# Attention with a top-31 threshold on one core: scores stored less a per-row constant, and the step between two counts taken out

## The reference, cut to what matters

```python
U = min(L, int(FACTOR * math.log(L)))            # 31
scores = jnp.einsum('bhqd,bhkd->bhqk', Q, K) / math.sqrt(D)
top_vals, _ = jax.lax.top_k(scores, U)
thresh = top_vals[..., -1:]
scores = jnp.where(scores < thresh, -jnp.inf, scores)
attn = jax.nn.softmax(scores, axis=-1)
context = jnp.einsum('bhqk,bhkd->bhqd', attn, V)
...
x = _layernorm(x + attention(x)); x = _layernorm(x + ffn(x))
```

## Time and profile before

| | us |
|---|---|
| median of 3 executions | 3479.99 (3476.94 to 3483.20) |
| profiled execution | 3479.86 |
| its span, first to last instruction | 3478.0 |
| granted TensorE clock, mean | 0.897 of full speed |

### The profile page before, as it was taken

The page is one execution under the profiler, slowest core; times in us unless marked ns, Lnnn a source line. Parts: engine busy times, 40 slices in busy tenths (PEclk is TensorE's granted clock), DMA queues, the critical chain, the costliest instruction groups (busy, mean ns, idle before and its releaser), DMA issues.

```text
span 3478.0 us, 83180 instructions
## 1 busy us (share of the span) xinstructions
PE 2872.5 (83%) x21439; PEld 1516.8 (44%) x21439; DVE 2716.7 (78%) x13407; ACT 2336.1 (67%) x5894; POOL 2372.2 (68%) x1549
## 2 busy tenths in 40 slices
PE   5889999697889888866998997988969887787886
PEld 2344545344444444433544453444535444343454
DVE  5888888788878877777887887887878877777861
ACT  3777777585767676655776776766757765576662
POOL 2777778576777766654777786776757765575782
PEclk6899999898999988887999998998979998899886
DMA  2101011110101111011010111101011110110000
GB/s 81 41 20 42 23 40 30 32 26 18 43 23 34 24 34 31 19 32 22 21 44 23 33 26 37 33 25 37 23 32 26 33 33 18 32 26 24 22 14 7
DMA packets 91073, 102.85 MB, mean 30 GB/s; under 512 B 34417, under 2 KB 52850, under 8 KB 90482
## 3 DMA queue, kind: packets, MB, share of 16 engines
q1 hardware_dynamic: 88448, 93.73, 11.2%
q10 hardware_dynamic: 2034, 2.76, 0.2%
HBM read 20.86 MB, written 8.39 MB: 8 GB/s over the span
## 4 chain that ended last, share of the span: by engine, by line
PE 42%; DVE 24%; issue 17%; ACT 9%; DVEq 5%; POOL 2%; SPq 1%; ACTq 1%; DMA 0%; POOLq 0%
DVE cand L855 7%; PE Y_ps L593 6%; PE bench L657 5%; PE bench L663 5%; PE Y_ps L590 4%; PE ctxT_ps L621 4%; PE ST_ps L607 4%; ACT junk L447 4%; PE ST_ps L604 3%; PE Y_ps L591 3%; DVE S L841 3%; DVEq L935 3%; ACT above L455 3%; DVE gtop L916 2%; PE bench L650 2%
## 5 line engine op out<-in xcount | busy, mean ns | idle before, releaser
L1073 POOL TENSOR_SCALAR mask<-S,thr,mb 128x512 bf16<-128x512 f32 x1024 | 2112.1, 2075 | 44.0 <-POOL mb L1067 34.9
L447 ACT ACTIVATE junk<-S,nt 128x512 bf16<-128x512 f32 x1024 | 733.7, 716 | 563.7 <-DVE S L841 549.4
L855 DVE MAX8 cand<-Y_ps 128x8 f32<-128x128 f32 x4096 | 1074.2, 283 | 0.4
L841 DVE TENSOR_SCALAR_CACHE_REDUCE S<-S_ps 128x512 f32<-128x512 f32 x1024 | 702.7, 686 | 275.5 <-PE S_ps L580 216.7
L590 PE MATMUL Y_ps<-ones_b,nbig 128*128 128x512 bf16 x1024 | 421.6, 412 | 521.4 <-DVE cand L855 330.3
L463 ACT ACTIVATE PT<-ST_ps 128x512 f32<-128x512 f32 x1024 | 595.9, 582 | 234.2 <-PE ST_ps L607 233.3
L455 ACT ACTIVATE above<-S,nt 128x512 bf16<-128x512 f32 x1024 | 726.4, 709 | 0.2 <-DVE nt L848 0.2
L1067 POOL TENSOR_SCALAR mb<-rmax 128x8 f32<-128x8 f32 x128 | 31.1, 243 | 894.8 <-DVEq L938 894.8
L580 PE MATMUL S_ps<-KS,QS 64*128 64x512 f32 x1024 | 540.3, 528 | 2.0 <-DMA KS<-Klo 1.4
L593 PE MATMUL Y_ps<-KS,QS 64*128 64x512 f32 x1024 | 539.9, 527 | 0.0
L604 PE MATMUL ST_ps<-QS,KS 64*128 64x512 f32 x1024 | 439.7, 429 | 29.0 <-ACT PT L463 27.2
(11 more groups left out here) (119 smaller groups left out, 4005.4 us busy)
## 6 DMA issues: line engine op xcount, KB each, us to landing
QS<-Qhi SPq DMA_DIRECT2D x512, 32.0 KB, 2.0
KS<-Khi SPq DMA_DIRECT2D x512, 32.0 KB, 2.0
KS<-Klo SPq DMA_DIRECT2D x512, 32.0 KB, 2.0
QS<-Qlo SPq DMA_DIRECT2D x512, 32.0 KB, 2.0
xTs<-in_xT SPq DMA_DIRECT2D x17, 512.0 KB, 3.7
xs<-in_x SPq DMA_DIRECT2D x16, 512.0 KB, 3.9
out<-xs SPq DMA_DIRECT2D x16, 512.0 KB, 2.9
hT<-in_wgT ACTq DMA_DIRECT2D x1, 768.0 KB
```

Of the source, the lines that this page charges most:

```text
L447: nc.scalar.activation(junk[:, :], S[:, score_place(j)[0], :], ACT.Sign, bias=nt0[:, hb, col:col + 1], accum_out=s0[:, j % 8:j % 8 + 1]).t ...
L841: nc.vector.tensor_scalar(S[:, at, :], S_ps[n % 2][:, :], 1.0, None, ALU.mult, op1=ALU.max, accum_out=rmax[:, n % RING:n % RING + 1]).then ...
L855: mx = nc.vector.max(cand[:, j % CANDS, i, :], Y_ps[j % 2][:, i * BW:(i + 1) * BW])
L1073: nc.gpsimd.tensor_scalar(mask[:, h % MASKS, t, :], S[:, score_place(j)[0], :], thr[:, r:r + 1], mb[:, r:r + 1], ALU.is_lt, op1=ALU.add).t ...
```

## The change

Scores are stored with the row constant `na` already added: evacuate becomes S = S_ps + na, `na` read as a per-partition operand in place of the immediate 1.0. `na` is the second threshold's constant part, so the first count needs a bias `nt0` that is a multiple of the deviation alone, and takes its input with a scale of -1. The second threshold test S + s0*nb + na > 0 becomes steep * S - (count) > 0: ScalarE's second count reads the per-row factor `steep` = 4 / (BETA * sd2) as its scale and the first count's own output `s0` as its bias. VectorE's `aim` is dropped. The lag of the second count goes from 3 to 2, its wait from `aimed_done` to `cnt0_done`; all later lags stay. `evacuate` now waits for `stat_done` at tiles 0 and 32 of a batch. VectorE's moments end with one more reciprocal (`rsd2`). As thresholds and masks must be in the same terms, `pick_threshold` writes its result to `least` and adds `na` of the 8 tiles into `thr` (one more VectorE instruction in 8 tiles, which `check` waits for), and GpSimd makes `mb` in two steps in place of one, rmax / 2^40 and then plus `back` = -na / 2^40. `first_thresholds` keeps five instructions, the last of which now also depends on the fourth.

```diff
-AIMED = 2
-COUNT1 = 3
+COUNT1 = 2
...
-                nc.scalar.activation(junk[:, :], S[:, score_place(j)[0], :], ACT.Sign, bias=nt0[:, hb, col:col + 1],
+                nc.scalar.activation(junk[:, :], S[:, score_place(j)[0], :], ACT.Sign, bias=nt0[:, hb, col:col + 1], scale=-1.0,
                                      accum_out=s0[:, j % 8:j % 8 + 1]).then_inc(cnt0_done, 1)
...
-                act.wait_ge(aimed_done, T - COUNT1 + 1)
+                hb, col = j // HALF_TILES, (j % NT) * HALF + j // NT % HALF
+                act.wait_ge(cnt0_done, T - COUNT1 + 1)
                 if not (first and n < COUNT1 + 4):
                     act.wait_ge(below_done, T - COUNT1 - 3)
-                nc.scalar.activation(above[:, j % 4, :], S[:, score_place(j)[0], :], ACT.Sign, bias=nt1[:, j % 8:j % 8 + 1],
-                                     accum_out=s1[:, j % RING:j % RING + 1]).then_inc(cnt1_done, 1)
+                nc.scalar.activation(above[:, j % 4, :], S[:, score_place(j)[0], :], ACT.Sign, bias=s0[:, j % 8:j % 8 + 1],
+                                     scale=steep[:, hb, col:col + 1], accum_out=s1[:, j % RING:j % RING + 1]).then_inc(cnt1_done, 1)
...
-                    nc.vector.tensor_tensor(sd2[:, :], sd0[:, :], sd1[:, :], ALU.add).then_inc(sd_done, 1)
-
-            def evacuate(T, n, first):
+                    m = mark(nc.vector.tensor_tensor(sd2[:, :], sd0[:, :], sd1[:, :], ALU.add))
+                    dve.wait_ge(dve_step, m)
+                    nc.vector.reciprocal(rsd2[:, :], sd2[:, :]).then_inc(sd_done, 1)
+
+            def evacuate(T, n, b, first):
+                hb, col = n // HALF_TILES, (n % NT) * HALF + n // NT % HALF
+                if n % HALF_TILES == 0:
+                    dve.wait_ge(stat_done, b * 2 + hb + 1)
...
-                nc.vector.tensor_scalar(S[:, at, :], S_ps[n % 2][:, :], 1.0, None, ALU.mult, op1=ALU.max,
+                nc.vector.tensor_scalar(S[:, at, :], S_ps[n % 2][:, :], na[:, hb, col:col + 1], None, ALU.add, op1=ALU.max,
                                         accum_out=rmax[:, n % RING:n % RING + 1]).then_inc(s_copied, 1)
...
-            def aim(T, n):
-                j = (n - AIMED) % TILES
-                hb, col = j // HALF_TILES, (j % NT) * HALF + j // NT % HALF
-                dve.wait_ge(cnt0_done, T - AIMED + 1)
-                nc.vector.tensor_scalar(nt1[:, j % 8:j % 8 + 1], s0[:, j % 8:j % 8 + 1], nb[:, hb, col:col + 1],
-                                        na[:, hb, col:col + 1], ALU.mult, op1=ALU.add).then_inc(aimed_done, 1)
...
-                t = mark(nc.vector.tensor_reduce(thr[:, r:r + PAIR], picked[:, :, :], AX.X, ALU.max))
+                t = mark(nc.vector.tensor_reduce(least[:, :], picked[:, :, :], AX.X, ALU.max))
...
+                picks["kept"] = mark(nc.vector.tensor_tensor(by_head(thr[:, r:r + PAIR]), by_head(least[:, :]), of_pair(na, g), ALU.add))
...
+                if "kept" in picks:
+                    dve.wait_ge(dve_step, picks["kept"])
                 dve.nop(nofuse=True).then_inc(thr_done, 1)
...
-                    nc.gpsimd.tensor_scalar(mb[:, r:r + PAIR], rmax[:, r:r + PAIR], 1.0 / BIG, None,
-                                            ALU.mult).then_inc(mb_done, 1)
-                    wait_apart(pool, mb_done, pair + 1)
+                    nc.gpsimd.tensor_scalar(rbig[:, :], rmax[:, r:r + PAIR], 1.0 / BIG, None, ALU.mult).then_inc(mb_done, 1)
+                    wait_apart(pool, mb_done, 2 * pair + 1)
+                    nc.gpsimd.tensor_tensor(by_head(mb[:, r:r + PAIR]), by_head(rbig[:, :]),
+                                            of_pair(back, (n - MASK) // PAIR % NP), ALU.add).then_inc(mb_done, 1)
+                    wait_apart(pool, mb_done, 2 * pair + 2)
...
+                nc.gpsimd.tensor_scalar(asd[:, :], sd2[:, :], -ZERO / 2, None, ALU.mult).then_inc(stat_step, 1)
+                nc.gpsimd.tensor_scalar(nt0[:, hb, :], sd2[:, :], -(ZERO - Z) / 2, None, ALU.mult).then_inc(stat_step, 1)
+                nc.gpsimd.tensor_scalar(steep[:, hb, :], rsd2[:, :], 4.0 / BETA, None, ALU.mult).then_inc(stat_step, 1)
+                wait_apart(pool, stat_step, n0 + 1)
+                nc.gpsimd.tensor_tensor(na[:, hb, :], nmean[:, :], asd[:, :], ALU.add).then_inc(stat_step, 1)
                 wait_apart(pool, stat_step, n0 + 4)
+                nc.gpsimd.tensor_scalar(back[:, hb, :], na[:, hb, :], -1.0 / BIG, None, ALU.mult).then_inc(stat_done, 1)
```

More of the change, by code:

```diff
@@ L37 @@
 BETA = SHRINK / (L * float(np.exp(-Z * Z / 2) / np.sqrt(2 * np.pi)))
+ZERO = Z2 + BETA * (L / 2 - EXPECTED)
 BLOCKS = 4
@@ L212, in build @@
         rsd = sb("rsd", [P, NT * HALF])
-        zsd = sb("zsd", [P, NT * HALF])
+        rsd2 = sb("rsd2", [P, NT * HALF])
         asd = sb("asd", [P, NT * HALF])
@@ L216, in build @@
         na = sb("na", [P, 2, NT * HALF])
-        nb = sb("nb", [P, 2, NT * HALF])
+        back = sb("back", [P, 2, NT * HALF])
+        steep = sb("steep", [P, 2, NT * HALF])
         V = sb("V", [P, NT, NG, VG])
@@ L237, in build @@
         mb = sb("mb", [P, RING])
+        rbig = sb("rbig", [P, PAIR])
         thr = sb("thr", [P, RING])
@@ L240, in build @@
         s0 = sb("s0", [P, 8])
-        nt1 = sb("nt1", [P, 8])
         above = sb("above", [P, 4, L], BF16)
@@ L248, in build @@
         picked = sb("picked", [P, PAIR, RANKS])
+        least = sb("least", [P, PAIR])
         hidden = sb("hidden", [P, PAIR])
@@ L281, in build @@
         cnt0_done = sem("cnt0_done")
-        aimed_done = sem("aimed_done")
         cnt1_done = sem("cnt1_done")
@@ L315, in build, with of_pair, by_head @@
         block = ctx.enter_context(nc.Block())
+        def of_pair(a, g):
+            h = 2 * g % HALF
+            return a[:, 2 * g // HALF, :].rearrange("p (t h) -> p h t", h=HALF)[:, h:h + 2, :]
+        def by_head(a):
+            return a.rearrange("p (h t) -> p h t", h=2)
         def wait_apart(eng, s, value):
@@ L899, in pick_threshold @@
             def pick_threshold(n):
-                g = (n - THRESHOLD) // PAIR
+                g = (n - THRESHOLD) // PAIR % NP
                 r, c = g * PAIR % RING, g % 2
@@ L903, in pick_threshold @@
                     dve.wait_ge(dve_step, picks["picked"])
-                t = mark(nc.vector.tensor_reduce(thr[:, r:r + PAIR], picked[:, :, :], AX.X, ALU.max))
+                t = mark(nc.vector.tensor_reduce(least[:, :], picked[:, :, :], AX.X, ALU.max))
                 dve.wait_ge(dve_step, t)
-                nc.vector.scalar_tensor_tensor(out=flag[:, c, 0:PAIR], in0=hidden[:, :], scalar=GONE, in1=thr[:, r:r + PAIR],
+                nc.vector.scalar_tensor_tensor(out=flag[:, c, 0:PAIR], in0=hidden[:, :], scalar=GONE, in1=least[:, :],
                                                op0=ALU.max, op1=ALU.is_gt,
                                                accum_out=flag[:, c, PAIR:PAIR + 1]).then_inc(flag_done, 1)
+                picks["kept"] = mark(nc.vector.tensor_tensor(by_head(thr[:, r:r + PAIR]), by_head(least[:, :]), of_pair(na, g), ALU.add))
             def general(j):
@@ L991, in slots @@
                             top_of_block(T, n, i)
-                    if due(AIMED, n, first, rest):
-                        aim(T, n)
                     for what, part in uses:
@@ L1012, in slots @@
                     if not rest:
-                        evacuate(T, n, first)
+                        evacuate(T, n, b, first)
                     for what, part in uses:
@@ L1078, in first_thresholds @@
                 n0 = G * 4
-                nc.gpsimd.tensor_scalar(zsd[:, :], sd2[:, :], -Z / 2, None, ALU.mult).then_inc(stat_step, 1)
-                nc.gpsimd.tensor_scalar(asd[:, :], sd2[:, :], -(Z2 + BETA * (L / 2 - EXPECTED)) / 2, None,
-                                        ALU.mult).then_inc(stat_step, 1)
-                nc.gpsimd.tensor_scalar(nb[:, hb, :], sd2[:, :], -BETA / 4, None, ALU.mult).then_inc(stat_step, 1)
-                wait_apart(pool, stat_step, n0 + 2)
-                nc.gpsimd.tensor_tensor(nt0[:, hb, :], zsd[:, :], nmean[:, :], ALU.add).then_inc(stat_step, 1)
+                nc.gpsimd.tensor_scalar(asd[:, :], sd2[:, :], -ZERO / 2, None, ALU.mult).then_inc(stat_step, 1)
[3 more added lines that the diff above has]
+                nc.gpsimd.tensor_tensor(na[:, hb, :], nmean[:, :], asd[:, :], ALU.add).then_inc(stat_step, 1)
                 wait_apart(pool, stat_step, n0 + 4)
-                nc.gpsimd.tensor_tensor(na[:, hb, :], nmean[:, :], asd[:, :], ALU.add).then_inc(stat_done, 1)
+                nc.gpsimd.tensor_scalar(back[:, hb, :], na[:, hb, :], -1.0 / BIG, None, ALU.mult).then_inc(stat_done, 1)
             def layer_norm(b, i):
```

## The result

The changed kernel takes 3384.39 us (median of 4, 3383.76 to 3385.19) against 3478.47 for the kernel before (median of 4): ratio 0.973, 95% interval 0.9713 to 0.9747, so 94 us less. Forecast were 3449 us and 31 less; the time lies outside the range of 3402 to 3498, on its fast side.

The account below looks back on a forecast made before the run. No engine is full; the end moves between TensorE, VectorE and ScalarE slot by slot. Terms along the chain of waits summed to -30.5 us, from 3479.9 to 3449 us; 8-in-10 range 3402 to 3498.

Parts of the forecast that it names:

- aim out: VectorE's aim goes: 0.17 us gained at each of 313 aims on the chain of waits, -53 us.
- second count a slot sooner, no factor: TensorE's `below` stops waiting for ScalarE's second count: 160 passages at 0.25 us, -40; at 0.35 without the factor, 56.
- factor (8 + 7, and 16 inside the -40): ScalarE's second count 0.09 to 0.1 us longer: +8 in 52 short slots, +7 at 69 passages leaving by the exponential.
- evacuation's operand: VectorE's evacuation reading a per-row operand: 0.065 us longer at 400 evacuations on the chain, +26 us.
- added step, reciprocal, start, GpSimd: VectorE's added step in 8 tiles +15 (58 at 0.25), reciprocal +2, first evacuation after the statistics +1.5, GpSimd's step +3.
- I expect 27 again, or one off: Exact search: 27 tiles searched as before, or one off, though values round otherwise; no term in the sum, no chance.
- The clock: TensorE's granted clock, left unchanged at 0.897; an effect there would make all of the forecast wrong.
- Its guard: TensorE's `turned`, waiting for ScalarE's exponential, is late next: 0.30 us to gain, 0.20 after the longer count.
- A: The exponential takes the second count's place in holding TensorE: +16 in place of -40, 3505 us; chance 0.15.
- B: Half the relief is given back to block maxima or TensorE's own work: -16, 3473 to 3480 us; chance 0.12.
- C: VectorE's added step collides with GpSimd's masks, 0.9 us a step: +38 more, 3487 us; chance 0.06.
- D: The evacuation's operand is free and each passage of the second count gains 0.38 us: 3402 us; chance 0.07.

Follow-up runs that it names:

- e5: e1 with VectorE's aim left out, second count taking the first threshold as bias and waiting for its tile's first count, lag 3: 3084.61 us.
- e1: The kernel before with the unsettled rows' flags always zero, so the exact search is left out: 3147.33 us.
- e8: e5 with the lag of the second count at 2 in place of 3: 3030.13 us.
- e2: The changed kernel with the exact search left out by flags that are always zero: 3094.40 us.
- e12: e2 with an immediate scale of 100.0 in place of the row's factor on the second count: 3070.29 us.
- e13: e2 with the evacuation's immediate 1.0 back in place of the row constant: 3077.92 us.
- e3: The kernel before, exact search kept, with an immediate scale of 1.0001 on the second count: 3448.86 us, 24 exact searches.
- e6: e1 with the evacuation's immediate 1.0 replaced by a per-row operand that holds 1.0: 3173.03 us.
- e4: e2 with the lag of the second count put back from 2 to 3, the aim still out: 3142.53 us.
- e11: e2 with VectorE's added step in 8 tiles issued twice, the second into an unused tile: 3123.29 us.

## Why the prediction was wrong, step by step

Single prices without the exact search, beside the terms of the prediction (us). The first two were measured from the kernel before, the next two out of the changed kernel, so the fifth row, what is then left, also holds whatever the edits do to each other:

| step | forecast | measured | from |
|---|---|---|---|
| aim out | -53 | -63 | e5 - e1 |
| second count a slot sooner, no factor | -56 | -54 | e8 - e5 |
| factor (8 + 7, and 16 inside the -40) | +31 | +24 | e2 - e12 |
| evacuation's operand | +26 | +16 | e2 - e13 |
| added step, reciprocal, start, GpSimd | +21.5 | +24 | what is left to e2 |
| sum | -31 | -53 | e2 - e1 |
| three exact searches fewer | 0 | -28 | e3 |
| not separated | | -13 | rest to -94 |

*What failed first* is the last paragraph of the rivals: "I expect 27 again, or one off; this hangs inside the range and gets no chance of its own." The term was left out of the sum, and no price was worked out for a call; at 9 to 12 us a call, three calls (28 us in e3) are nearly as large as the whole forecast of 31, and without them the time would have been some 3412 us, inside the range. The price could have been read: the stretch of a call in the timeline of the kernel before is 12.8 us. The words "the test compares values shifted alike" were right in exact arithmetic, but a test for sign is where a last bit decides, and the change turned a plain sum into a multiply-add.

*The clock* was the other thing held fixed. Granted were about 0.900 before (0.897 in the profiled execution) and 0.913 after, some 110 us less at the lower level. Over 88 executions on record (every experiment's, and the kernel before in the same jobs), each against the mean of its own kernel and job, the time moves by about 0.25 us for each us at the lower level. By that, an estimate, some 27 of the 94 us came by way of the clock. They are no row beside the others but a part of them, and no run holds the clock fixed, so that it follows the time and does not make it is not excluded.

*The aim* was right in kind, and its step of 0.17 us doesn't contradict what the prediction cites against it: the same section (the Trainium skill, "VectorE: DVE Perf Modes", "The DRAIN you can't avoid") adds that an operation which is not held back starts earlier. The term was short by 10: 1024 x 0.17 would be 174, and 63 are 370 of those, where the chain showed 313. The chain is one path of several that lie close together, and the clock rose with the edit; which of the two the 10 us are is not shown.

*The operand* was priced right (+26 on the kernel before, exactly as said) but is worth 16 once the aim is out (12 counted within its job), presumably because VectorE is then less often last. The terms were all read off one trace and added up as if the others weren't there. The difference of 10 us is little more than the spread of these runs (13 us within e6).

*The factor* had the right price for one (0.093 us) and nearly the right sum. ScalarE's light slots became 1.98 us long as said, while VectorE's take 1.81 and not 1.98; the +8 for the meeting of the two is neither borne out nor refuted.

*The slot* was the best of the terms, -54 against -56 without the factor, and 48 (e4 against e2) where it said 40. The 0.25 us a passage was a choice between 0 and 0.38, so the size is in part luck. Its guard, that `turned` would be late next at 0.30 us, named one of two next waits: the block maxima took back 69 us and `turned` 51 (e5 to e8).

*The added step* was priced low for its part: +29 for one more in e11, where the prediction took 0.25 us at 58 places. Why is open (e11), and so is whether the first such step costs what the second does. The other small terms were not measured apart; the table's remainder of 24 holds them together with the 11 us of the flag's operation, which the prediction had put at nothing, and is itself a difference across jobs.

*The last 13 us* stay open. The 24 calls that both have cost 12.6 us each in e3 (3448.86 - 3147.33) and 12.1 in the changed kernel, which would be 12 us, but says the same thing over again; the spread of e3 alone is 12 us, and no run takes the two apart.

*The rivals.* A is out by e8. B is out as a time, but the block maxima did take back a part of the relief, as it says. C is out for the added step by e11, while the operation ahead of it lasts 11 us longer in sum. D had the mechanism of the slot right, at 0.34 us a passage (54 / 160), but its other leg, a free operand, is not so. The range failed for lack of a case in which the data-dependent path changes: with the three searches back the time would have been inside it.

## What to carry to other kernels

Where a kernel has a slow path that data switch on, read its price from the time between the neighbouring instructions, not from its own, and ask of each edit to the arithmetic whether it moves a value across the test. Terms read from one chain of waits are good for each edit alone to some 10 to 15 us here; that those on the engine that got relief shrink once several are made together rests on one case, the operand. Look at the granted clock of every run before prices are compared, and add up a wait over the matmuls that share it before it is compared between traces, for some records can be missing. And where an engine works through a fixed list in each slot, put first what the next engine waits for and needs nothing recent itself: two lines moved were worth 59 us on the changed kernel and 70 on the kernel before.

## What the runs showed of the hardware that was not expected

- A branch on a value read into a register costs more than the work behind it: 6.6 to 7.8 us in which VectorE has no instruction, ahead of the exact search and behind it together, for 5.4 us of work (stretches with one call); e1 puts a call at 12.2 us, so nothing of it is seen to hide.
- TensorE's granted clock is at its lower level for 10 to 24 us around each exact search of the kernel before, in which TensorE stands (9.81 us in the call shown); a slot's first matmul then takes 0.59 us and not 0.39.
- VectorE's 128x8 flag operation, with two SBUF inputs, lasts 169 ns in the median and up to 1402; all 46 slow ones of 128 in either kernel began while GpSimd was in an instruction.
- An immediate scale of 1.0001 on ScalarE's second count, which costs it no time (709 ns with and without), removed three of 27 exact searches (e3). That exact zeros in the sum of signs had caused them is inferred.
- A per-row scale adds 93 ns to a 128x512 activation that already has a per-row bias (709 to 802), and a per-row operand in place of an immediate 59 ns to VectorE's evacuation from PSUM (686 to 745 in e6).
